# One GpSimd order, one ScalarE order and one register load in a four-layer kernel

## The reference, cut to what matters

```python
x = x + attn_a(ln(x), ...)     # linear attention, 4 heads
x = x + ffn(ln(x), ...)        # 8 experts, each token goes to one of them
x = x + attn_b(ln(x), ...)     # sparse attention, below
x = x + ffn(ln(x), ...)        # the same experts again

def attn_b(x):                 # B=16, S=256, D=128, 4 index heads of 64
    Q, K, V = split(x @ w_qkv.T + b_qkv); Q, K = rope(Q), rope(K)
    iq, ik, iw = x @ w_iq.T + b_iq, x @ w_ik.T + b_ik, x @ w_iw.T + b_iw
    head_scores = relu(einsum('bqhd,bkd->bhqk', iq, ik))
    index_scores = einsum('bhqk,bqh->bqk', head_scores, iw)
    mask = the 32 largest index_scores of each row
    attn = softmax(Q @ K.T / sqrt(D) where mask, else -inf)
    return attn @ V @ w_o.T + b_o
```

## Time and profile before

| | us |
|---|---|
| median of three runs | 567.39 |
| the profiled execution | 566.95 |
| its span | 565.1 |
| TensorE busy in the span | 451.0 (80%) |
| VectorE busy | 380.0 (67%) |
| ScalarE busy | 337.2 (60%) |
| GpSimd busy | 288.4 (51%) |

### The profile page before, as it was taken

The page is one execution under the profiler, slowest core; times in us unless marked ns, Lnnn a source line. Parts: engine busy times, 40 slices in busy tenths (PEclk is TensorE's granted clock), DMA queues, the critical chain, the costliest instruction groups (busy, mean ns, idle before and its releaser), DMA issues. The chain is left out here.

```text
span 565.1 us, 11633 instructions
## 1 busy us (share of the span) xinstructions
PE 451.0 (80%) x3048; PEld 390.7 (69%) x3048; DVE 380.0 (67%) x1501; ACT 337.2 (60%) x934; POOL 288.4 (51%) x329
## 2 busy tenths in 40 slices
PE   1789985859999986999889998889647668786991
PEld 1578865859999874676666766667437568676981
DVE  5789976425666622999999999999957234434661
ACT  1568852226776616889999899998521245434650
POOL 5753440454430025987778777775410633665442
PEclk9989995979999989999999999999756969888996
DMA  8942232131331110011111111110111321121110
GB/s 224 288 135 77 74 90 25 44 88 53 99 87 35 34 34 15 9 37 32 28 30 30 42 44 28 30 30 21 36 35 5 84 57 48 56 64 56 39 36 17
DMA packets 45070, 32.42 MB, mean 57 GB/s; under 512 B 13524, under 2 KB 39508, under 8 KB 45012
## 3 DMA queue, kind: packets, MB, share of 16 engines
q1 hardware_dynamic: 39892, 19.11, 12.2%
q0 software_dynamic: 5120, 12.62, 8.5%
HBM read 19.10 MB, written 12.62 MB: 56 GB/s over the span
## 5 line engine op out<-in xcount | busy, mean ns | idle before, releaser
L629 PE MATMUL bank<-X,w 128*128 x624 | 91.0, 292 | 18.3 <-ACT X L834 16.3
L639 PE MATMUL bank<-WE,hT 128*128 x624 | 89.2, 289 | 14.3 <-ACT hT L847 6.8
L427 POOL DMA_INDIRECT big<-rows,gidx x64 | 61.5, 961 | 74.7 <-DVE gidx L1147 28.2
L629 PEld LDWEIGHTS bank<-X,w 128*128 128x128 f32 x624 | 82.0, 205 | 22.3 <-issue 21.9
L639 PEld LDWEIGHTS bank<-WE,hT 128*128 128x128 f32 x624 | 81.3, 203 | 17.0 <-issue 16.9
L834 ACT ACTIVATE X<-bank 128x128 f32<-128x128 f32 x64 | 17.9, 280 | 94.6 <-PE bank L620 60.9
L1179 DVE TENSOR_SCALAR hT<-bank,w 128x128 f32<-128x128 f32 x156 | 47.6, 346 | 39.0 <-issue 12.2
L660 PE MATMUL bank<-xbT,WB 128*128 128x256 f32 x224 | 59.2, 394 | 13.2 <-ACT xbT L872 8.5
L839 ACT ACTIVATE w<-WE 128x644 f32 x78 | 57.5, 738 | 3.1 <-DVE big L1191 2.8
L847 ACT ACTIVATE hT<-bank,w 128x128 f32<-128x128 f32 x156 | 48.7, 367 | 13.4 <-PE bank L629 10.1
L447 POOL DMA_INDIRECT X<-x,pidx x32 | 31.7, 989 | 48.7 <-DMA x<-big 41.2
(11 more groups left out here) (161 smaller groups left out, 1026.6 us busy)
## 6 DMA issues: line engine op xcount, KB each, us to landing
WE<-w_experts SPq DMA_DIRECT2D x2, 2048.0 KB, 11.5
rows<-xf SPq DMA_DIRECT2D x32, 128.0 KB, 2.2
rows<-X SPq DMA_DIRECT2D x32, 128.0 KB, 2.7
X<-x SPq DMA_DIRECT2D x4, 512.0 KB, 7.6
x<-big SPq DMA_DIRECT2D x32, 64.0 KB, 1.5
big<-rows,gidx POOLq DMA_INDIRECT x64
WB<-w_idx SPq DMA_DIRECT2D x1, 640.0 KB, 5.7
WE<-b SPq DMA_DIRECT2D x1, 512.0 KB, 12.9
```

Source lines behind the costliest of these rows:

```text
L427: pool.indirect_dma_start(xg[:, j, :], None, rows_dram[n], bass.IndirectOffsetOnAxis(ap=gidx[:, j:j + 1], axis=0)).then_inc(f["g"][j % G_R ...
L629: mm = pe.matmul(bank[r + 2 * (k // 2)][:, k % 2 * P:(k % 2 + 1) * P], w1[st.slot(1, 4)][:, k * P:(k + 1) * P], moving, start=True, stop=True)
L639: mm = pe.matmul(bank[4 + r][:, 0:D], hT[r][:, k, :], WE[:, bass.ds(expert[(s - 2) % TURN], 1), W2_AT + k * D:W2_AT + (k + 1) * D].rearran ...
```

## The change

Three parts.

1. `opens` returns nothing beyond step T = 32, so that VectorE's load at step 40 is gone, in both expert stages. The other engines' loops have no load there.
2. GpSimd's step in the sparse attention is written in another order: first the gather of item s+3, then the power for what VectorE took at its step s-1, then the bias, then cosine and sine, `qr`, and both head sums last. The power for step s used to stand behind the head sums of step s, and the gather behind it. The last step's bias no longer stands in a row behind the last head sum.
3. ScalarE evicts v after `iw` and `xb`, instead of before.

```diff
         def opens(st, lag):
-            return (st.base - HEAD) % TURN == 0 or st.base == lag or st.base == T
+            return st.base <= T and ((st.base - HEAD) % TURN == 0 or st.base == lag or st.base == T)
...
             for s in range(B + 2):
                 b, r = s, s % 2
+                if b + 3 < B:
+                    gather_x(b + 3)
+                if s > 0:
+                    inverse_std(s - 1)
                 if b < B:
+                    pool.wait_ge(b_["xb"], b + 1)
+                    pool.tensor_tensor(X[:, b * C:(b + 1) * C, :], X[:, b * C:(b + 1) * C, :],
+                                       bo_bc[:, :].unsqueeze(1).to_broadcast([P, C, D]), ALU.add).then_inc(b_["xo"], 1)
                     pool.wait_ge(b_["pje"], 8 * b + 7)
...
-                    add_heads(b, r, 0)
                     pool.wait_ge(b_["rp"], 2 * (b + 1))
                     after(pool, b_["S"], C * (b - 1))
                     pool.tensor_tensor(qr[r][:, :, :], qk[r][:, 0:2, :], qk[r][:, 2:4, :], ALU.add).then_inc(b_["qr"], 1)
+                    add_heads(b, r, 0)
                     add_heads(b, r, 1)
-                inverse_std(s)
...
-                if b + 3 < B:
-                    gather_x(b + 3)
+            inverse_std(B + 1)
...
-                def projected(pair):
+                def projected(pair, which=(0, 1)):
                     act.wait_ge(b_["pj"], 5 * b + pair + 1)
-                    for i in (2 * pair, 2 * pair + 1):
+                    for i in (2 * pair + w for w in which):
...
                 if st.on(0, B):
-                    projected(3)
+                    projected(3, (0,))
...
                 if st.on(-1, B):
                     normalise_b(st, -1)
+                if st.on(0, B):
+                    projected(3, (1,))
```

## The result

The changed kernel takes 584.2 us in the median (581.55 to 585.53), where before took 567.3 in the same call. The ratio of the runs is 1.028 (95% interval 1.023 to 1.033): slower by 2.8%; the two medians lie 16.9 us apart. The forecast was 565.7 us, in a range of 562.6 to 568.6. It was wrong, in sign and by far in size.

The account below looks back on a forecast made before the run. Bound by VectorE's load before the last expert tile and attention's ScalarE-TensorE loop; -3.05 (loads) + 1.5 (clock) + 0.3 (start) - 0.4 (end) = -1.65 us, giving 565.7 us, range 562.6 to 568.6.

Parts of the forecast that it names:

- Part 1, the loads: Ends of both expert stages: without VectorE's load the last tile comes 1.57 and 1.48 us earlier, 3.05 us gained.
- The clock: TensorE behind the 60 transposes: gap grows to 4.04 us, clock falls, first attention projections at half rate, +1.5 us.
- Rival B: TensorE's clock holds over the 4.04 us gap behind the transposes: sum -3.15, 564.2 us; chance 0.22.
- Part 3, v last: ScalarE in the sparse attention: idle 0.88 us per step moves from before `vb` to before relu; value 0.
- `vb` late: ScalarE in the sparse attention: the downside case of v last, referred to Part 2 without a size there.
- Part 2: GpSimd's order: later power makes VectorE wait 0.9 us, within its slack; value 0 in steps 2 to 15.
- `nb` comes at 358.74 + 0.66: Steady attention step: `nb` at 359.40, then `xb`, `vb`; ScalarE free about 360.5 for relu at 361.43, 0.9 us to spare.
- Rival D: Sparse attention: GpSimd, through power, `nb`, `xb`, `vb` and relu, becomes the loop; +5 to +11 us, 570.7 at +5; chance 0.13.
- Start and end: Sparse attention: step 1 loses 0.3 us by `vb` and late `nb`; step 16 gains 0.4 as GpSimd's bias runs earlier.

Follow-up runs that it names:

- e11_load_order: The changed kernel without Part 3, v evicted in its old place: 1.0162 of before (1.0116 to 1.0207), 576.8 us.

## Why the prediction was wrong

- *Part 1, the loads: right.* 1.57 and 1.48 us forecast; the last `yb` starts with TensorE, the last scatters are 1.48 us closer, and alone it measured what it was to give with the clock term, -1.5 us.
- *The clock: right.* Forecast were a gap of 4.04 us, a lost clock and +1.5 us; the trace shows 3.98, 0.75 over the stretch and +1.36. Rival B is out.
- *Part 3, v last: right alone (1.000), wrong in company.* The prediction named "`vb` late" as the case in which it costs, and then gave it no price, because Part 2 said that `nb` had 0.9 us to spare.
- *Part 2: here it failed,* at the step "`nb` comes at 358.74 + 0.66". It moved `xf` and `nb` by the lateness of the power, but let them keep the durations that they had beside gathers. It did not ask what GpSimd does at their new time. Behind the power there now come bias, cos and sin at once, with no wait between them. From the start of `xf` to the end of `nb` it took 3.1 us instead of 0.66, so 0.9 us of spare time became a delay of some 1.6. The lateness itself did fit, as the kernel with the wait showed (0.69 us left).
- *Rival D had the right loop and the wrong price.* It put the meetings at the head sum and the gathers, and its losses at most at 0.55 us each; the trace of before held a `wk` of 1.03 us beside `qr`, where the next such `wk`, at 354.85, took 0.48. The difference is not a price for a meeting; it follows from what was left of `qr` when the `wk` arrived. `qr` is in GpSimd's timeline of before:

```profile
352.39 1.27 POOL L488 TENSOR_TENSOR qr<-big 128x512 f32<-128x512 f32 x1
```

The `wk` began at 352.90, with 0.76 us of `qr` still to run.
- *Start and end.* In the first steps +0.3 us was forecast (bounds 0.1 and 0.6). From the first projection to the first `prT` the changed kernel took 0.70 us more than the loads alone (26.17 against 25.47, one execution of each), above the bound. In step 16, -0.4 was forecast: both L1283 take 0.48 us, and the last period is 10.00 instead of 10.41 us.
- *The low clock inside the attention* was not thought of. It goes with the late steps: in the seven kernels whose steady periods are 11.82 to 11.84 us the clock was full from the first `prT` to 400 us, and it fell inside the attention in five of the six that have late steps (the sixth is e11_load_order).

The trace of the changed kernel shows holding to the end: in its late steps `xf` and `nb` end within 0.1 us behind one of GpSimd's operations, whatever their own size. The Trainium skill (SBUF — State Buffer, Who interferes with whom) has this as a rule. The port pair that VectorE and GpSimd share is an exclusive lock, taken for the whole instruction by whichever issues first. It is wanted by a VectorE instruction with two inputs in SBUF (`nb`), against a GpSimd operation that reads SBUF, and by a `tensor_scalar` in its two-port mode (which `xf` can be; no run here shows its mode, nor the ports themselves). The prediction weighed only the weaker sentence that it cites, that the two contend, and priced it as a slowdown; by the rule, each meeting costs up to the whole GpSimd operation, here 0.7 to 1.3 us, and the new order has three in a row. The trace agrees with the rule, and the 3.13 us of an `nb` go beyond a single operation.

## What to carry to other kernels

When an instruction of VectorE or GpSimd is moved, list what the other engine runs at its new time, not only what it waits for. Here an instruction of VectorE that reads two tensors, though it writes two numbers a partition, cost the whole of the GpSimd operation beside it. If it stands on the path of others, put it beside a pause or behind a wait, even at the price of starting later. Spare time of 0.9 us is no cover for a meeting with 1.3 us operations, and an edit that measures zero alone (v last) may not be zero when another has used up the slack.

## What the runs showed of the hardware beyond that

- An instruction that is held over one GpSimd operation can be held over the next ones too: `nb` took 0.15 us free, 0.68 behind the bias, 1.24 behind sin, 3.13 behind bias, cos and sin together. Neighbouring steps of one loop differed by up to 3.8 us in period, and where the hold went over three operations the start of `nb` was the same within 0.02 us as where it ended behind one.
- A pause on GpSimd of some 0.9 us a step (the added wait) cost nothing and gave back 3.2%.
- GpSimd's gathers held `xf` but not `nb`. With the power ahead of the gathers, an `xf` that began 0.05 us into the second gather took 0.34 us, one that began 0.3 into it 0.87, and one that began 0.5 into it 0.65. In before, an `xf` that began 0.6 us into the first gather took 0.46 and ended 0.02 behind it. An `nb` that began 0.14 us into a gather of 0.95 us (at 240.35 in before) took 0.15 us, as when free.
- Behind the transposes TensorE's clock was kept over gaps of 1.28 to 2.65 us (five kernels) and lost over 3.90 to 4.16 us (all eight kernels that had such a gap). But a gap of 2.42 or 2.50 us ahead of the transposes lost it, in the three kernels that had one, so the length of the gap alone does not decide. Where the first projections kept it with 84 transposes, it was lost one step later in one execution and not in another.
- Inside the attention no length of idle time parts the falls from the rest. In the changed kernel it fell behind the sixth wait in a row of 1.1 to 1.3 us, and then twice behind a single wait of 1.15. With the power ahead of the gathers it fell behind two waits of 1.26 and 1.31 us and not behind three in a row of 1.27 to 1.30. With half of cos and sin it fell once with no idle time over 0.4 us in the 20 us before.
